# A graph network's attention on one core: VectorE's loops over sixteen groups a turn in place of eight

## The reference

```python
def _gat_layer(x, src, dst, W, a_src, a_dst, b, heads, ch, concat):
    n = x.shape[0]
    h = (x @ W).reshape(n, heads, ch)
    alpha_src = jnp.sum(h * a_src, axis=-1)
    alpha_dst = jnp.sum(h * a_dst, axis=-1)
    e = alpha_src[src] + alpha_dst[dst]
    e = jnp.where(e > 0, e, NEG_SLOPE * e)
    alpha = _segment_softmax(e, dst, n)
    msg = h[src] * alpha[:, :, None]
    out = jax.ops.segment_sum(msg, dst, num_segments=n)
    out = out.reshape(n, heads * ch) if concat else out.mean(axis=1)
    return out + b
```

## Time and profile before

| | us |
|---|---|
| median of three runs | 8928.67 |
| the runs | 8913.6, 8929.7, 8928.67 |
| the profiled execution | 8916.15 |
| its span in the trace | 8914.5 |
| layer one's loops, about | 4190 to 6420 |
| layer two's loops, about | 6690 to 8830 |

### The profile page before, as it was taken

How to read it: one execution, slowest core, us unless ns; L and a number is a source line. 1 busy time by engine, 2 the same in 40 slices (tenths; PEclk the granted TensorE clock), 3 DMA queues, 4 the chain that set the end, 5 groups by cost and what they waited for, 6 DMA issues and landing times.

```text
span 8914.5 us, 232214 instructions
## 1 busy us (share of the span) xinstructions
PE 6375.9 (72%) x50562; PEld 5197.4 (58%) x50563; DVE 6392.5 (72%) x27688; ACT 4848.8 (54%) x11854; POOL 6136.1 (69%) x7562
## 2 busy tenths in 40 slices
PE   2466666666599999985777777777647777777775
PEld 2366656665588888863444444444445665556664
DVE  7799833333267767757999999999957777777776
ACT  4133333333245555535767667677647777777775
POOL 0377777777777777735777777777637777777775
PEclk9988888888799999986888888888755555555555
DMA  4232222222233333312222222222521111111114
GB/s 141 52 63 62 62 63 62 63 62 62 60 92 85 86 86 85 86 30 59 55 54 55 54 54 55 55 54 54 49 23 28 28 28 28 28 28 28 28 28 27
DMA packets 990660, 491.49 MB, mean 55 GB/s; under 512 B 830674, under 2 KB 841604, under 8 KB 990276
## 3 DMA queue, kind: packets, MB, share of 16 engines
q0 software_dynamic: 168832, 302.29, 15.6%
q1 hardware_dynamic: 701892, 169.48, 10.4%
q10 hardware_dynamic: 119840, 18.68, 1.3%
HBM read 356.53 MB, written 151.48 MB: 57 GB/s over the span
## 4 chain that ended last, share of the span: by engine, by line
issue 25%; DVE 20%; PE 19%; POOL 18%; DMA 7%; ACT 6%; DVEq 3%; ACTq 1%; POOLq 0%; SPq 0%
POOL z_s L637 13%; POOL arena L687 5%; DMA arena<-table,arena 5%; PE ps_all L959 5%; PE ps_all L969 5%; PE ps_all L982 3%; ACT arena L823 3%; PE ps_all L979 2%; DVE shift L1528 2%; DVE arena L1487 2%; DVE arena L1532 2%; PE ps_all L1066 1%; ACT arena L855 1%; DVE arena L1573 1%; DMA z_s<-arena 1%
## 5 line engine op out<-in xcount | busy, mean ns | idle before, releaser
L687 POOL DMA_INDIRECT arena<-table,arena x3616 | 3471.7, 960 | 1504.4 <-issue 982.6
L637 POOL DMA_INDIRECT z_s<-arena x1660 | 1592.1, 959 | 849.9 <-issue 477.5
L1090 PE MATMUL ps_all<-arena 128*128 128x132 f32 (+1 forms) x7232 | 1561.4, 384 | 1.8 <-DVE acc L1590 1.8
L1090 PEld LDWEIGHTS ps_all<-arena 128*128 128x128 f32 x7232 | 1384.9, 284 | 2.7 <-issue 2.6
L823 ACT ACTIVATE arena<-lanes_b,arena 128x128 bf16<-128x128 bf16 x3616 | 1147.1, 387 | 415.6 <-DVE arena L1461 414.4
L1487 DVE TENSOR_REDUCE arena<-ps_all 128x2 f32<-128x1024 f32 x904 | 1098.9, 1216 | 15.5 <-PE ps_all L1107 15.5
L1066 PE MATMUL ps_all<-ident_b,arena 128*128 128x128 bf16 x3616 | 472.3, 273 | 789.1 <-DMA arena<-table,arena 522.6
L1107 PE MATMUL ps_all<-arena,pick 128*128 128x512 bf16 x2260 | 971.0, 523 | 72.5 <-DVE arena L1487 72.1
L847 ACT ACTIVATE arena<-ps_all 28x512 bf16<-28x512 bf16 (+1 forms) x904 | 522.6, 578 | 718.5 <-PE ps_all L1066 718.5
L742 ACT ACTIVATE arena<-ps_all 18x512 f32<-18x512 f32 x415 | 243.3, 586 | 1212.0 <-PE ps_all L946 1192.5
L1066 PEld LDWEIGHTS ps_all<-ident_b,arena 128*128 128x128 bf16 x3616 | 291.1, 120 | 942.7 <-DVE arena L1474 528.8
(11 more groups left out here) (259 smaller groups left out, 16141.0 us busy)
## 6 DMA issues: line engine op xcount, KB each, us to landing
arena<-z_s SPq DMA_DIRECT2D x452, 264.0 KB, 2.7
arena<-table,arena POOLq DMA_INDIRECT x3616
arena<-rec_d SPq DMA_DIRECT2D x1660, 10.0 KB
z_s<-arena POOLq DMA_INDIRECT x1660
rec_d<-in_rec ACTq DMA_DIRECT2D x1, 16160.0 KB, 58.8
arena<-ids_d SPq DMA_DIRECT2D x904, 4.0 KB
arena<-pos_d SPq DMA_DIRECT2D x830, 0.5 KB
arena<-pos_d ACTq DMA_DIRECT2D x830, 0.5 KB
```

Of the source, the lines that this page charges most:

```text
L637: pool.indirect_dma_start(z_s, bass.IndirectOffsetOnAxis(ap=slot[:, g.slot(SLOTS), u:u + 1], axis=0), z_out[:, g.slot(SLOTS), u, :], None) ...
L687: pool.indirect_dma_start(g_rows[:, r, u * step + CODE_WORDS:(u + 1) * step], None, tables[n], bass.IndirectOffsetOnAxis(ap=ids[:, r, 0, u ...
L1090: mm = pe.matmul(ps[6][:, 0:out_w], a_hot_f[:, g.slot(4), u, :], g_msg[:, g.slot(4), u * out_w:(u + 1) * out_w], start=(u == 0), stop=(u = ...
```

## The change

VectorE alone, in both attention layers, gets a loop body of sixteen steps in place of eight, and the load at the head of a turn brings 3 * SLOTS = 24 registers in place of 2 * SLOTS = 16 (eight back, sixteen on). The loop runs 27 times in place of 54; peel and rest stay as they are. The other four engines keep their loops of eight.

```diff
--- before.py
+++ after.py
@@ -147,9 +147,9 @@
     return slice(PART_AT[k], PART_AT[k] + PARTS[k])
 
 
-def attention_pipeline(eng, depth, step, layer, each_round=None):
-
-    pipelined(eng, GROUPS, depth, step, layer * GROUPS, peel=2 * SLOTS, unroll=SLOTS, each_round=each_round)
+def attention_pipeline(eng, depth, step, layer, each_round=None, unroll=SLOTS):
+
+    pipelined(eng, GROUPS, depth, step, layer * GROUPS, peel=2 * SLOTS, unroll=unroll, each_round=each_round)
 
 
 class Chain:
@@ -1443,7 +1443,7 @@
                 dve.sem_inc(S("table_ready"), 1)
 
                 step = CODE_WORDS + row
-                buckets = Rounds(dve, mybir.EngineType.DVE, bucket_of, NT - 1, SLOTS, 2 * SLOTS)
+                buckets = Rounds(dve, mybir.EngineType.DVE, bucket_of, NT - 1, SLOTS, 3 * SLOTS)
 
                 def edge_codes(g):
 
@@ -1600,7 +1600,7 @@
                     for part in (shifts, codes, shifts):
                         next(part, None)
 
-                attention_pipeline(dve, 8, attend, n, buckets.load)
+                attention_pipeline(dve, 8, attend, n, buckets.load, unroll=2 * SLOTS)
                 dve.wait_ge(S("a_added"), GROUPS * (n + 1))
                 link(dve.tensor_scalar(rs, ac[:, :, :, ch], 1e-16, None, ALU.add))
                 link(dve.reciprocal(rs, rs))
```

## The result

The changed kernel takes **8981.05 us** (median of four runs, 8979.11 to 8985.09) against 8925.21 for the kernel before (four runs, 8913.6 to 8929.7): ratio 1.0062, 95% interval 1.0050 to 1.0074. It is slower by 56 us, and the forecast was 8977.

What follows compares the result with a forecast made beforehand. VectorE's own loop was taken to bound layer one, GpSimd's gathers layer two. Per turn of sixteen -1.91 + 0.5 + 3.2 = +1.79 us; x 27 = +48.3 on 8928.67 gave 8977 us, range 8915 to 9045.

Steps and rivals of the forecast that it cites:

- Layer one is VectorE's, and a turn's end lies open there: Layer one: VectorE is late only through its own loop; nothing covers a turn's end of 1.91 us.
- 27 ends at 1.91 us: Layer one, VectorE: 27 turn ends of 1.91 us go, 51.6 us less.
- The load, +0.5: Layer one, turn's head: loading 24 registers instead of 16 costs 0.5 us more a turn, 13.5 us in all.
- The jump, 3.2 us, between 2.2 and 4.2: Layer one, each turn's jump back: VectorE stands 3.2 us until its code is fetched again; ends 2.2 and 4.2.
- rival B: At the jump back: a short stand, one packet only, price 1.4 to 2.0 us, 8937 us; chance 0.10.
- GpSimd's jump: At the start, GpSimd skips the edge-sorting branch: stand read as 2.2 us (second packet a look-ahead) or 4.2 (both needed).
- Walking on through the long body costs nothing.: Layer one's loop body: running straight through the longer code adds zero.
- What holds 331 rows may not hold 651: Layer one's loop grows from 331 to 651 compiled rows; its code likelier doesn't stay in the store.
- Layer two, nothing: Layer two: GpSimd paces it and VectorE's 5.2 us turn end is under the 10 us cover, so zero.
- A: Rival for the jump back: the code stays or is read ahead, price zero, -38 us, 8891 us; chance 0.15.
- C: Rival: two stands a turn, +135 us (9063), or layer two uncovered too, +97 us (9025); chance 0.13.

Runs made afterwards that it cites:

- load24: The kernel before, eight groups a turn, with its load alone of 24 registers in place of 16: 8957.04 us, ratio 1.0032.
- load12: The kernel before with its load of 12 registers in place of 16: 8914.01 us, ratio 0.9984.
- slot100: The kernel before with the first instruction of VectorE's two attention loops placed at slot 100 of a block of 256: 9107.6 us, ratio 1.0202.
- hint: The changed kernel plus one instruction a turn announcing the closing branch of VectorE's two attention loops: 8944.63 us, ratio 1.0019 to the kernel before.
- slot0: The kernel before with the heads of VectorE's two attention loops placed at slot 0 of a block: 8899.47 us, ratio 0.9994.
- two_again: The kernel before with sixteen groups and 24 registers in layer two alone, repeated on another chip: 8908.94 us, ratio 1.0002.
- e_two: The kernel before with sixteen steps and 24 registers in layer two alone, on a chip where before took 12002.42: 12054.04 us, ratio 1.0037.
- e_one: The kernel before with sixteen steps and 24 registers in layer one alone, on a chip where before took 12002.42: 12091.36 us, ratio 1.0080.
- e_long: The kernel before with fourteen extra wait instructions behind each L1487 of layer one's loop, where before took 12002.42: 12147.86 us, ratio 1.0129.

## Why the prediction was right

*Layer one is VectorE's, and a turn's end lies open there.* Right. load24 and load12 move the time by what they change at the head, slot100 by what it adds there.

*27 ends at 1.91 us.* Nearly. In before the last group of a turn takes 6.70 us and the others 5.06 in the medians of all turns, so an end that goes is worth 1.64. The 1.91 took the mean of five groups in one turn, 5.03, for all eight.

*The load, +0.5.* Right: 1.61 in place of 1.10.

*The jump, 3.2 us, between 2.2 and 4.2.* The mechanism was right, the size 0.6 too high: 2.62 us by L1513 in the changed kernel, 2.63 in slot100. The reading of GpSimd's jump by which the second packet is a look-ahead, 2.2, was the nearer one: VectorE runs from 5015.57 us, and its second packet starts at 5016.20. The middle of the two readings was no measurement, and the part of it that waits for both pieces was wrong. hint shows that the stand is a fetch. The price is over rival B's 1.4 to 2.0.

*"Walking on through the long body costs nothing."* This is the term that failed. The fifteen groups of a turn that don't end it take 76.52 us, 5.10 each against 5.06: +0.6 us a turn, or 16 us over 27. About half of it is seen: VectorE's idle time outside the turn's start is 0.45 us a turn of sixteen, against 0.15 a turn of eight before, with small stops (0.03 to 0.11 us) at five places 15 us apart, just ahead of a packet. The other half is busy time, which differs as much between other kernels of this study, and stays open. (In slot100 such stops are 0.25, 0.24 and 0.12 us.) Stops so small can't be told from the gaps of up to 0.09 us in the straight group that the prediction looked at the earlier trace rows.

So by the turn: -1.64 + 0.51 + 2.62 + 0.58 = +2.07, against +2.17 measured, and 27 x 2.17 = 59 us where the forecast had 48. That the median came within 4 us of the forecast is partly luck: the 0.6 too much for the jump and the 0.6 too little for the body cancel, and between the two profiled executions it is 63 us, between the medians 56 us.

*What holds 331 rows may not hold 651.* Right: 7 and 8 packets a turn, where before has none. But the length alone doesn't decide. The 356 instructions of slot100's loop, places 100 to 455, were fetched (5 packets a turn), and the same 356 at places 0 to 355 in slot0 were not. The measurement says that code comes in pieces of 128, and all runs fit three of them for the loop. Where between place 356 (slot0, kept) and 456 (slot100, not) the limit lies was not tried.

*Layer two, nothing.* Right: +5.7 us from step 448 to 895 in the changed kernel, +7.2 in slot100 with its 54 stands, and a ratio of 1.0002 in two_again. It holds where GpSimd sets the pace: on the chip of e_two the same change in layer two lost 52 us.

*Rivals.* A (the code stays) fell by the packets. B had the mechanism, VectorE goes on after one packet, but not the price: L1513 at 4.47 us. C fell with layer two and with one stand a turn. hint made A in part true, and even so sixteen a turn stays 17 us behind eight: with the fetch hidden, the end saved is paid back by the load, by the body's 0.6 us a turn, and by the two loop exits.

## What to carry to other kernels

Unrolling saved a turn's end of 1.64 us here and cost a stand of 2.62, since the loop's code was no longer kept. In a loop of VectorE count all the compiled instructions, waits and register work too, and keep them within three pieces of 128, with the head placed so that they are: 356 in three pieces fetched nothing in layer one's loop but one packet (slot0), 356 in four pieces 5 a turn, for 2% (slot100). That 257 fit wherever the head is, and up to 384 if it begins a piece, is an estimate from these pieces; no run tried it. Look for packets on the instruction queue inside a loop: before has none in layer one, and where they came in layer one the price was at the first instruction of the turn, 2.62 us in the changed kernel and 2.63 in slot100. And load no more registers at the head than a turn uses: each costs 63 ns there, and four fewer gave 15 us.

## What was not expected of the hardware

- The same loop, moved by some places, went from no packets to 5 a turn and cost 2%. An edit far ahead in the program can do that: e_one and e_long made an untouched loop fetch.
- In hint, where the announced jump isn't taken, VectorE stands for 14 to 15 us once, at the loop's exit; in layer one some 10 us of it reached the end (from +1.7 at step 440 to +11.8 at step 447).
- A register load did not run beside VectorE's own reduction, in the one place where it was tried: it was over 1.34 us after the reduction's end, though eleven registers at the head would have taken about 0.8 by estimate (0.85 for twelve).
